# Hybrid attention megakernel on one core: fixed places for the steps, two causal layers side by side at the start, and one PSUM bank for each reading instruction

## The reference

```python
x = x + _L0_attn_a_ref(_layernorm(x), Wq, Wk, Wv, Wo)        # causal, 16 heads of 16, rotary positions
x = x + _L0_ffn_ref(_layernorm(x), Wg, Wq, Wk, Wv, Wo)       # gated: attention over half the rows
x = x + _L0_attn_b_ref(_layernorm(x), w_qkv, w_out, rel_bias) # 16 heads of 64, relative bias
x = x + _L0_ffn_ref(_layernorm(x), Wg, Wq, Wk, Wv, Wo)
```

## Time and profile before

| | us |
|---|---|
| median of the runs shown (2449.46 to 2453.07) | 2450.35 |
| the profiled execution | 2451.99 |
| its span, first to last instruction | 2450.3 |
| PE busy | 2231.9 |
| VectorE, ScalarE, GpSimd busy | 1308.7, 1131.7, 524.9 |
| mean granted clock of TensorE | 0.986 |

### The profile page before, as it was taken

One profiled execution on the slowest core, in us unless ns is written; L12 is line 12 of the kernel. 1 busy time (PEld: TensorE's weight loads), 2 busy tenths in 40 slices (PEclk: granted clock), 3 DMA queues, 4 the chain that ended last, 5 costly groups with the idle time before them and its releaser, 6 DMA issues.

```text
span 2450.3 us, 38728 instructions
## 1 busy us (share of the span) xinstructions
PE 2231.9 (91%) x15600; PEld 1335.0 (54%) x15616; DVE 1308.7 (53%) x3536; ACT 1131.7 (46%) x2033; POOL 524.9 (21%) x755
## 2 busy tenths in 40 slices
PE   5779899898999989999999999999999999998996
PEld 3444556554565535655466554665546654565564
DVE  4446544656536556456555565554663656546334
ACT  2224555445435554355452555425543455435552
POOL 2101312122302312022311123111321112301220
PEclk9889999999999999999999999999999999999998
DMA  3001011111001200112011110112010111001100
GB/s 116 1 1 35 31 44 65 44 65 40 23 24 49 71 28 22 38 50 67 16 38 35 55 49 16 44 35 70 29 37 23 50 55 44 23 22 50 67 22 9
DMA packets 28913, 98.16 MB, mean 40 GB/s; under 512 B 2752, under 2 KB 11328, under 8 KB 28608
## 3 DMA queue, kind: packets, MB, share of 16 engines
q1 hardware_dynamic: 28736, 95.70, 11.4%
HBM read 91.49 MB, written 4.19 MB: 39 GB/s over the span
## 4 chain that ended last, share of the span: by engine, by line
PE 75%; DVE 17%; ACT 4%; issue 2%; DMA 1%; POOL 0%; SPq 0%
PE ps L584 21%; PE ps L958 9%; PE ps L1201 9%; PE ps L1187 8%; PE ps L1194 8%; DVE mcol L896 4%; DVE probs L915 4%; DVE mcol L828 4%; PE ps L1026 3%; PE ps L1002 3%; PE ps L1143 3%; PE ps L1130 2%; PE ps L1040 2%; ACT PTc L698 2%; PE ps L1111 1%
## 5 line engine op out<-in xcount | busy, mean ns | idle before, releaser
L736 ACT ACTIVATE probs<-probs,peak 128x512 f32<-128x512 f32 x512 | 364.9, 713 | 395.0 <-DVE peak L921 395.0
L667 POOL TENSOR_SCALAR probs<-probs,rtotal 128x512 f32<-128x512 f32 x512 | 343.3, 692 | 819.3 <-DVE rtotal L925 819.3
L915 DVE CUSTOM_DVE_ANT_0 probs<-ps,band 128x512 f32<-128x512 f32 x512 | 332.7, 687 | 180.9 <-PE ps L1187 180.2
L743 ACT ACTIVATE PT<-ps 128x1024 f32<-128x1024 f32 x256 | 254.1, 1018 | 87.4 <-PE ps L1194 86.8
L1187 PE MATMUL ps<-KT,QT 64*128 64x512 f32 x1024 | 278.6, 635 | 8.4 <-DVE mcol L896 4.2
L1194 PEld LDWEIGHTS ps<-ident,probs 128*128 128x128 f32 x2048 | 224.9, 141 | 89.1 <-issue 83.7
L1194 PE MATMUL ps<-ident,probs 128*128 128x128 f32 x2048 | 264.8, 276 | 3.9 <-DVE mcol L896 2.3
L828 DVE TENSOR_REDUCE mcol<-ps 128x2 f32<-128x1024 f32 (+3 forms) x256 | 194.6, 817 | 97.3 <-PE ps L1006 96.4
L584 PE MATMUL ps<-xnT,wb 128*128 128x512 f32 x512 | 234.9, 599 | 3.0 <-DMA wb<-in_w_b 2.6
L1201 PE MATMUL ps<-PT,Vb 128*64 128x512 f32 x1024 | 233.8, 598 | 1.2 <-ACT PT L743 1.2
L698 ACT ACTIVATE PTc<-ps 128x768 f32<-128x768 f32 (+1 forms) x192 | 157.0, 882 | 89.8 <-PE ps L1026 89.8
(11 more groups left out here) (125 smaller groups left out, 3007.8 us busy)
## 6 DMA issues: line engine op xcount, KB each, us to landing
band<-in_band SPq DMA_DIRECT2D x64, 896.0 KB, 4.6
wb<-in_w_b SPq DMA_DIRECT2D x64, 384.0 KB, 3.0
x<-in_x SPq DMA_DIRECT2D x8, 512.0 KB, 3.8
out<-x SPq DMA_DIRECT2D x16, 256.0 KB, 2.2
wob<-in_wo_b SPq DMA_DIRECT2D x1, 1024.0 KB, 7.1
wqk<-in_wqk_a SPq DMA_DIRECT2D x1, 512.0 KB, 4.5
wva<-in_wv_a SPq DMA_DIRECT2D x1, 256.0 KB, 4.1
woa<-in_wo_a SPq DMA_DIRECT2D x1, 256.0 KB, 4.2
```

The lines of the kernel that those rows point to most:

```text
L667: last = g.tensor_scalar(unit, unit, rtotal[:, r % 8, e:e + 1], 1.0, ALU.mult, ALU.mult)
L736: last = a.activation(unit, unit, ACT.Exp, bias=peak[:, r % 8, e:e + 1], accum_out=total[:, r % 8, e:e + 1])
L743: a.activation(PT[:, k % 2, :, :, tile_of(q)], bank(now).rearrange("p e (k n) -> p e k n", k=NT), ACT.Copy).then_inc(act_read, 1)
L915: last = v.tensor_tensor_reduce(out=probs[:, r % ROWS_HELD, e, :], in0=bank(now)[:, e, :], in1=band[:, k % 2, e, lo:lo + T], scale=1.0, sc ...
```

## The change

Five things are changed together.

1. Every unit of PSUM has one bank and is read by one instruction. c_p1, c_p2, f_p1 and f_p2 have four units, c_xt, b_xt, c_t1, b_row and b_tr two. f_rank, which had two units, is split into the steps f_rank and f_spread.
2. b_val is cut into four steps and b_y's two into two parts each. A part can be placed alone; the bank stays open until the last one.
3. in_order() no longer chooses by the expected times. Each step has a place, a number in the table PLACE (one row for the cycle, others for the first two samples and the last two), and the ready step with the lowest number comes next. The expected times, with new values, now only choose the banks.
4. The causal layers of samples 0 and 1 have memory of their own (causal and gated memory number 1 lies over the biased layer's buffers), so both can be under way at the start. b_k of sample 0 comes after causal layer 1. Gated layer 3 of sample 7 uses the second memory too.
5. The loads and constants stand at the head of the main block and not in a block before it; x is loaded in halves, and each first use waits for its own load.

```diff
-Unit = namedtuple("Unit", "bank banks reader no freed")
+Unit = namedtuple("Unit", "banks reader no freed")
...
-    "c_p1": [("o", "dve", 2), ("o2", "dve", 2)], "c_m": [("o", "dve", 1)],
-    "c_p2": [("o", "act", 2), ("o2", "act", 2)], "c_val": [("o", "act", 1)],
+    "c_p1": [(f"o{h}", "dve", 1) for h in range(4)], "c_m": [("o", "dve", 1)],
+    "c_p2": [(f"o{h}", "act", 1) for h in range(4)], "c_val": [("o", "act", 1)],
...
-    "b_row": [("o", "dve", 2)], "b_tr": [("o", "act", 2)], "b_val": [("o", "dve", 1)], "b_y": [("o", "dve", 1)],
+    "b_row": [("o", "dve", 1), ("o2", "dve", 1)], "b_tr": [("o", "act", 1), ("o2", "act", 1)], "b_val": [("o", "dve", 1)], "b_y": [("o", "dve", 1)],
...
+PARTS = {"c_val": 3, "b_val": 4, "b_y": 2}
...
+CYCLE = 2819
+PLACE = {
+    ("cycle", "b_k"): [940, 564, 782, 1543, 1850, 2107, 2827, 2871],
...
+def turn(x):
+
+    row, cycle = stage(x)
+    return PLACE[row, x.kind][x.n * SEVERAL.get(x.kind, 1) + x.q] + CYCLE * cycle
...
-        for x in ready:
-            if xn_held and x.kind in ("c_ln", "f_ln", "b_ln"):
-                continue
-            engine = work[x][0][0]
-            start = max([free[engine]] + [done[y] + wait for y, wait in needs[x]])
...
-            key = (max(start, free["pe"] + 0.1) - EARLY.get(x.kind, 0), -chain[x])
-            if best is None or key < best[0]:
-                best = key, x, start
-        _, x, t = best
+        x = min((x for x in ready if not (xn_held and x.kind in ("c_ln", "f_ln", "b_ln"))), key=lambda x: (turn(x), number[x]))
...
+    causal = [add(causal_steps(s), [], []) for s in range(2)]
+    entered = [add(ffn_steps(0, 1), causal[0], [])]
+    side = add(ffn_steps(1, 1), causal[1], entered[0])
+    entered.append(side)
     for s in range(B):
...
+        if s == 0:
+            layer = [(x, a, b + causal[1] * (x.kind == "b_k" and x.n == 0)) for x, a, b in layer]
...
                         if kind == "c_p2":
                             _, w = c_p2_parts(q)
-                            for i, name in enumerate(("o", "o2")):
+                            for h, name in enumerate(names(now)):
                                 act.wait_ge(act_full, plan.unit(now, now, name))
-                                a.activation(pt_c(q)[:, 2 * i:2 * i + 2], bank(now, name)[:, :, 0:w],
-                                             ACT.Exp).then_inc(act_read, 1)
+                                a.activation(pt_c(m, q)[:, h], bank(now, name)[:, 0:w], ACT.Exp).then_inc(act_read, 1)
...
-                            a.activation(PT[:, k % 2, :, :, tile_of(q)],
-                                         bank(now).rearrange("p e (k n) -> p e k n", k=NT),
-                                         ACT.Copy).then_inc(act_read, 1)
+                            for e, name in enumerate(names(now)):
+                                act.wait_ge(act_full, plan.unit(now, now, name))
+                                a.activation(PT[:, k % 2, e, :, tile_of(q)],
+                                             bank(now, name).rearrange("p (k n) -> p k n", k=NT),
+                                             ACT.Copy).then_inc(act_read, 1)
...
                         if kind == "f_p2":
                             c, e = n // 2, n % 2
                             read(now, Step("f_m", s, l, n))
-                            room(now)
-                            room(now, "o2")
-                            o = head_banks(now)
+                            for name in names(now):
+                                room(now, name)
+                            o = [bank(now, name) for name in names(now)]
...
                         if kind == "b_row":
                             read(now, Step("b_q", s, l, n))
                             read(now, Step("b_k", s, l, n))
-                            room(now)
-                            for e in range(2):
-                                last = te.matmul(o[:, e, :], QT2[half(e), k % 2, tile_of(q)], KT2[half(e), k % 2, :],
-                                                 start=True, stop=True)
+                            for e, name in enumerate(("o", "o2")):
+                                room(now, name)
+                                full(te.matmul(bank(now, name), QT2[half(e), k % 2, tile_of(q)], KT2[half(e), k % 2, :],
+                                               start=True, stop=True), now, name)
+                            continue
```

More of the change, by code:

```diff
@@ L136 @@
-EARLY = {
-    "b_k": -0.5, "b_ln": 0.25, "b_v": -0.57, "b_xt": 2.17, "b_y": 0.44, "c_ln": 0.15, "c_m": 0.5, "c_ot": 1.06,
-    "c_p1": 0.5, "c_p2": 2.06, "c_qk": 1.11, "c_rot": 0.64, "c_t1": 0.5, "c_turn_k": 0.5, "c_turn_q": 0.5,
-    "c_v": 0.89, "c_val": 0.5, "c_xt": 0.67, "c_y": 0.77, "f_gate": 1.71, "f_gather": 1.51, "f_k": 0.54, "f_ln": 0.69,
-    "f_m": 0.65, "f_o": 0.25, "f_p1": 0.61, "f_p2": 1.25, "f_q": 0.35, "f_rank": 1.28, "f_row": 0.53, "f_t1": 0.53,
-    "f_v": 0.74, "f_val": 0.73, "f_y": 0.65,
+CHANGE, PE_OUT, SIGNAL, HAND_OVER = 0.1, 0.2, 0.07, 0.06
@@ L313, in in_order @@
+        emptied = {"act": [], "dve": []}
+        ends = []
+        for i, op in enumerate(work[x]):
+            engine, us = op[:2]
+            if i:
+                j = op[2] if len(op) > 2 else i - 1
+                before = work[x][j][0]
+                t = ends[j] + (0 if before == engine else PE_OUT if before == "pe" else SIGNAL)
+            t = max(t, free[engine]) + us
             free[engine] = t
-            if i and engine != "pool":
+            ends.append(t)
+            if i and engine in emptied:
@@ L315, in in_order @@
                 emptied[engine].append(t)
-        if work[x][0][0] == "pe":
-            tiles = TILES.get(x.kind, 0) if x.kind != "c_p1" else 0
-        done[x] = t
-        for i, (name, reader, banks) in enumerate(UNITS.get(x.kind, ())):
-            opened = x._replace(q=0) if x.kind == "c_val" else x
-            at = banks_of[x, name] = banks_of[opened, name] if opened in done and opened != x else spot(banks)
-            for b in range(at, at + banks):
-                bank_free[b] = emptied[reader][min(i, len(emptied[reader]) - 1)] + SIGNAL
-                if x.kind == "c_val" and x.q < 2:
-                    bank_free[b] = 1e9
-                bank_used[b] = len(order)
+        done[x] = max(ends)
@@ new lines, in _ @@
+                            for e, name in enumerate(names(now)):
+                                room(now, name)
+                                for t in range(NT):
+                                    last = te.transpose(bank(now, name)[:, tile_of(t)],
+                                                        probs[:, r % ROWS_HELD, e, tile_of(t)], ident[:])
+                                full(last, now, name)
+                            continue
+                        if kind == "b_val":
+                            if q == 0:
+                                read(now, Step("b_tr", s, l, n, NT - 1))
+                                read(now, Step("b_v", s, l, n))
+                                room(now)
+                            for e in range(2):
+                                last = te.matmul(o[half(e), :], Vb[:, k % 3, q, half(e)], PT[:, k % 2, e, q, :],
+                                                 start=(q == 0), stop=(q == NT - 1))
+                            if q < NT - 1:
+                                continue
```

949 lines of the change are left out of this document (594 added, 355 removed).

## The result

| | before | after |
|---|---|---|
| median, us | 2450.15 | 2244.03 |
| lowest to highest | 2449.46 to 2453.07 | 2242.19 to 2247.84 |
| profiled execution, span | 2451.99, 2450.3 | 2247.84, 2246.0 |

A forecast was written before the change was run, and what follows sets the result against it. PE was taken to bound the cycles, and chains of short steps both ends. To the end of biased layer 0 374, six cycles 1706, biased layer 7 186 and the tail 62 gave 2328 us; range 2283 to 2400.

The forecast's parts named there:

- Array tilings: In PE's steps, each change of array tiling costs 0.17 us; a cycle has 93 changes in place of 122.
- Work in a cycle: PE's busy time without tiling changes is 255.6 us a cycle, so 271.4 with the new order's changes, before 276.3.
- Idle in a cycle: PE's idle time falls from 18.6 to 12.5 us a cycle, not below about 6; four-bank waits stay.
- The wait for wb: b_k of pair 7 waits for its wb refill in each cycle: 0 to 1.5 us, taken as 0.5.
- Split reads: One-bank reads add at most 99 us on ScalarE and 62 on VectorE over the kernel, covered by PE in the cycles.
- rival 4: Split reads show where PE waits for ScalarE, each adding 168 ns; all 99 us gives 2427 us; chance 0.05.
- The start: Before biased layer 0: first matmul 9, work 146, tiling changes 12.8, idle 19, clock loss 4, sum 191 us.
- Biased layers 0 and 7: The stretches of the first and last biased layers take 183 us (idle 9.1) and 186 us.
- The tail: Last gated layer alone: same chain with slightly longer split reads, 62 us for 61.0.
- Rival 3: The new order is tighter: idle 6 us a cycle and 8 at the start, 2276 us; chance 0.08.
- Rivals 1 and 2: PSUM-room waits stay, idle 18.6 a cycle, 2362 us, chance 0.22; start stays thin, idle 40, 2353 us, chance 0.12.
- Rival 5: Batches of four outrun their readers, up to 3.1 us a pair over 64 pairs: +198, 2526 us; chance 0.04.

The follow-up runs named there:

- two_bank: Changed kernel's order kept, but c_p1, c_p2, f_p1, f_p2, b_row and b_tr back in units of two banks, read as before the change; 2355.9 us.
- lazy_room: Changed kernel, but c_p1, c_p2, f_p1 and f_p2 wait for each head's bank just before its first matmul, not for all four at once; 2238.0 us.
- late_adjacent: Changed kernel with its order and one-bank reads, but paired banks stand side by side and neither is freed before both are read; 2348.3 us.
- greedy: Changed kernel, but the next step is chosen by earliest start less EARLY, as in the kernel before, instead of by fixed places; 2500.7 us.
- alternated: Changed kernel with neighbouring runs of b_row, b_tr and b_val steps taken in turns wherever dependencies allow; 2334.5 us.
- change_cost: Changed kernel with 64 identity matmuls added in the last gated layer, on the whole array, on 64 rows, then alternating; 0.184 us a change.
- warm_tail: Changed kernel with 45 and 30 unread identity transposes put into PE's two longest waits in the last gated layer; 2245.3 us.
- all_three: Changed kernel with per-head bank waits, unread transposes in the last gated layer, and f_t1 and f_ot placed apart; 2224.9 us.

## Why the forecast was too high

The sum went by stretches, so the miss can be read stretch by stretch: start -9, biased layer 0 -4, six cycles -65, biased layer 7 -8, tail +4, together -82 of 2328. The mechanism, fewer waits and fewer changes of tiling in cycles that PE bounds, was right; the two terms of the cycle were mis-sized.

- **Array tilings: right.** 0.17 us a change was forecast, 0.184 measured for one kind of change. The counts come from the order. two_bank, with the banks of before and 93 changes for 122, is busy 269.1 us for 276.3: 7.2 less, of which 29 changes at 0.184 explain 5.3.
- **Work in a cycle: the term that was mis-sized.** I took the 276.3 us for which PE was busy, less 122 changes, as work: 255.6, and so 271.4 after. It is 267.0. The price of a change doesn't explain it (with 0.184 the forecast would be 271.0). What I called work held short waits, as three kernels with the same matmuls show: two_bank and the changed kernel have the same order and changes, and 269.1 against 267.0 busy; lazy_room has 270.6 in a cycle that is shorter. The forecast treated busy as a floor that no change of banks could touch. (The Trainium skill, Perfetto Trace Analysis, Identifying the Most-Contended Engine, says that the busy share of matmuls doesn't tell how close a kernel is to its limit, because they are pipelined. The runs here give that a size: 3.6 us of 270 between the changed kernel and lazy_room.) How much of the 276.3 was waiting before can't be read from them; only that 4.4 us more of it went than the changes of tiling explain.
- **Idle in a cycle: the other term that was mis-sized.** 12.5 us were forecast, at a floor of about 6; it is 6.6. I held that four-bank steps would still wait since they ask for all four at once. They wait 3.8 us in a cycle. For two_bank, which shares the order, the lines of such waits that are shown come to 12.1, and its idle time is still 18.7. So the order alone, though it covers most of the wait for Qzf (3.1 us before, 0.6 in two_bank), took nothing off the idle time of a cycle; with single banks it fell by 12. The reason that I gave for single banks, a read of 593 ns in place of 1018, was the smaller half of it: keeping a bank until its pair is read costs 57 us, needing two neighbours 71, both 104. The second I had not named at all.
- **The wait for wb: smaller.** 0.5 us a cycle was forecast; no wait for it is listed in the cycle shown, and one of 0.8 us in the whole trace. The "5.0 at worst" beside that term was low: on the chain that ended last in the kernel before, these loads take 4.9 to 5.2 us in the cycles and 5.8 once, at 2220 us.
- **Split reads: right, and rival 4, with the Trainium skill's rule, wrong here.** ScalarE's busy time rose from 1131.7 to 1163.5 us, 32 and not up to 99, which is 2.8% and less than the 5 to 10% given as a sign, since neighbouring reads overlap; no wait on it is longer than 0.8 us in the cycle shown; and with the banks' state held the same, one read or two can't be told apart (late_adjacent). The Trainium skill's advice in Advanced Engine Details and Errata, The Read-Write Bubble, to read several banks with one instruction means units of two banks here, and these cost 112 us in this order; the long read by itself neither costs nor gains anything measurable. Its other rule, that engines which aren't saturated but make others wait may do better with smaller instructions (Perfetto Trace Analysis, Optimizing Scalar/DVE Operations), held only where the smaller read also let a bank go: late_adjacent has the same short reads as the changed kernel but gives banks back in pairs, and takes 2348.3 us for 2244.0.
- **The start: right in kind.** First transposes of biased layer 0 at 182.4 us for 191. The first matmul came at 7.1 for 9, idle after it was 20.2 for 19, the clock 0.99, so that of the 4 us for it hardly any were lost, and work and changes were 155.1 for 158.8.
- **Biased layers 0 and 7: idle.** I gave both the idle time of the like stretch before, 9.1 us. They have 2.6 and 2.9, with 176.5 and 174.7 us busy for 173.8 and 177.
- **The tail: the clock.** 65.7 us for 62, at 0.73 for 0.89; PE is busy 44.2 us for 36.7 and idle 21.5 for 24.3. The profiled execution is the longest of the four, so part of the 4 us may be its own; two_bank's profile has 65.2 at 0.76.

Rival 3, the tighter order with 6 us idle a cycle, had the right mechanism and 2276 us (by its own numbers 2278: idle at the start falls from 19 to 8, by 11 and not 13). I gave it 0.08 and let the range leave half of it out; with the busy time as a floor even it ended 32 us too high. Rivals 1 and 2 had the right questions (does the room wait stay, does the start stay thin) and both were answered no. Rival 5 did not come: PE's waits for GpSimd's probs come to 0.4 us in the whole trace. In greedy, 257 us slower, they come to 16.

## What to carry to other kernels

When PE is the bound and PSUM is full, give each reading instruction a bank of its own, but only together with an order made for it: here the order gained 98 us (57 of it ahead of the cycles, where two causal layers now run side by side), single banks alone nothing, both 206. Before changing the order of steps, see what each engine that works in order then has in front of it: in alternated one layer norm that waited for its x held up PE. Don't take PE's busy time as a floor: compare two kernels with the same matmuls before calling it work. A wait that disappears from the list need not disappear from the time (3.8 us of waits, 0.6 us of cycle); the length of a repeating cycle is the measure.

## What the runs showed of the hardware

- A change between the whole array and 64 rows costs 0.184 us between two matmuls that take 0.232 each (change_cost).
- Where a step waits by head instead of at its front, the listed waits go and PE's busy time grows: 3.8 us and 3.6 us in a cycle of 273 (lazy_room). The mean of one matmul stays the same, 526 ns for 530.
- Two ScalarE reads of 512 columns, 617 ns each by their mean, overlap: 512 of them keep it busy 263.5 us, 256 reads of 1024 columns (1026 ns) 248.1.
- PE's granted clock in the last 66 us differs between kernels that have the same steps there: 0.73, 0.78 and 0.83 in three profiles, with 65.7, 62.3 and 61.6 us. With transposes put into its waits it was 0.91 in warm_tail and in all_three.
- One instruction that reads two PSUM banks and two that read one each come to the same total when the banks are taken and freed alike: 2355.9 and 2348.3 us (two_bank, late_adjacent), with ratios to the kernel before whose intervals overlap.
